# Attention on one Trainium2 core: a pair's eight sums over keys, in one group or in two

## What is computed

```python
sim = jnp.einsum('bhid,bhjd->bhij', qn, kn)            # 4 heads of 64, 1024 queries, 1101 keys
sim = jnp.where(full_mask[:, None, None, :], sim, neg)
attn = jax.nn.softmax(sim.astype(jnp.float32), axis=-1).astype(sim.dtype)
out = jnp.einsum('bhij,bhjd->bhid', attn, v)
out = out.transpose(0, 2, 1, 3).reshape(b, nl, INNER)
return out @ W_out + b_out
```

## Time and profile before

| | us |
|---|---|
| median of three runs | 876.07 |
| the three runs | 872.5, 883.99, 876.07 |
| profiled execution, first to last instruction | 875.4 |
| TensorE busy in it | 802.4 |
| VectorE busy | 546.3 |
| GpSimd busy | 373.1 |
| ScalarE busy | 366.9 |

### The profile page before, as it was taken

The page is one execution under the profiler, slowest core; times in us unless marked ns, Lnnn a source line. Parts: engine busy times, 40 slices in busy tenths (PEclk is TensorE's granted clock), DMA queues, the critical chain, the costliest instruction groups (busy, mean ns, idle before and its releaser), DMA issues.

```text
span 875.4 us, 13801 instructions
## 1 busy us (share of the span) xinstructions
PE 802.4 (92%) x4270; PEld 612.4 (70%) x4271; DVE 546.3 (62%) x1173; ACT 366.9 (42%) x1175; POOL 373.1 (43%) x396
## 2 busy tenths in 40 slices
PE   6888799999999899989999999999998799999995
PEld 4555445555555555548888878888886689999994
DVE  4958765777677756675998667777766433333331
ACT  4457133544354332344444366776660032222220
POOL 7256553344447364345475044444442312222221
PEclk9999599989899988999999999999998799999998
DMA  8580000000000000003600093000001364555520
GB/s 303 170 307 35 1 0 1 1 1 0 1 1 1 0 1 1 0 1 111 255 1 0 1 301 104 12 19 13 14 12 61 101 266 176 182 180 176 174 80 3
DMA packets 31887, 67.14 MB, mean 77 GB/s; under 512 B 3103, under 2 KB 22909, under 8 KB 30813
## 3 DMA queue, kind: packets, MB, share of 16 engines
q1 hardware_dynamic: 28699, 56.17, 18.3%
q0 software_dynamic: 2560, 10.17, 3.6%
q10 hardware_dynamic: 578, 0.19, 0.1%
HBM read 54.74 MB, written 12.68 MB: 77 GB/s over the span
## 4 chain that ended last, share of the span: by engine, by line
PE 67%; DVE 17%; issue 6%; ACT 3%; POOL 3%; DMA 2%; DVEq 0%; SPq 0%; ACTq 0%; POOLq 0%
PE PS L2105 9%; PE PS L2093 9%; PE PS L1488 7%; PE PS L734 6%; PE PS L1468 6%; PE PS L1296 5%; PE PS L1274 3%; PE PS L725 3%; PE PS L771 3%; PE PS L701 3%; PE PS L726 2%; DVE row_best L846 2%; PE PS L743 2%; POOL rrms L551 2%; ACT pc L1670 1%
## 5 line engine op out<-in xcount | busy, mean ns | idle before, releaser
L1055 ACT ACTIVATE EX<-PS 128x512 f32<-128x512 f32 x144 | 78.9, 594 | 133.4 <-PE PS L726 130.6
L846 DVE TENSOR_REDUCE row_best<-PS 128x1 f32<-128x1024 f32 x64 | 77.8, 1221 | 41.8 <-PE PS L701 41.5
L1015 POOL TENSOR_TENSOR sumP<-sumP,EX 128x1024 f32<-128x1024 f32 x32 | 75.7, 2364 | 43.1 <-ACT EX L1055 42.7
L1670 ACT ACTIVATE pc<-PS,mx 128x77 f32<-128x77 f32 x256 | 78.8, 359 | 26.8 <-DVE mx L1565 26.8
L2093 PEld LDWEIGHTS PS<-xeT,w 128*128 128x128 f32 x736 | 85.6, 192 | 3.6 <-DMA w<-in_L_ffn_W 1.3
L2093 PE MATMUL PS<-xeT,w 128*128 128x128 f32 x736 | 86.1, 275 | 2.0 <-DMA w<-in_L_ffn_W 1.1
L2105 PE MATMUL PS<-w,heT 128*128 x368 | 83.3, 379 | 1.3 <-DVE oe L2035 1.3
L2132 POOL DMA_INDIRECT out<-oe,target x23 | 23.2, 1011 | 126.1 <-DVE oe L2035 126.1
L734 PE MATMUL PS<-EX,V 128*64 128x512 f32 (+1 forms) x288 | 76.5, 640 | 0.0
L2105 PEld LDWEIGHTS PS<-w,heT 128*128 128x128 f32 x368 | 68.1, 190 | 10.0 <-issue 1.7
L1488 PE MATMUL PS<-vw,pcT 128*128 128x256 f32 (+1 forms) x320 | 73.0, 383 | 1.2 <-ACT pcT L1683 1.2
(11 more groups left out here) (283 smaller groups left out, 1716.1 us busy)
## 6 DMA issues: line engine op xcount, KB each, us to landing
w<-in_L_ffn_W SPq DMA_DIRECT2D x31, 1024.0 KB, 10.1
vw_rows<-vwn SPq DMA_DIRECT2D x2, 1232.0 KB
kwH_rows<-kwH SPq DMA_DIRECT2D x1, 2464.0 KB, 7.4
kwL_rows<-kwL SPq DMA_DIRECT2D x1, 2464.0 KB, 13.7
kwH<-kwH_rows POOLq DMA_DIRECT2D x1, 2464.0 KB, 12.3
kwL<-kwL_rows POOLq DMA_DIRECT2D x1, 2464.0 KB, 19.2
vw<-vw_rows SPq DMA_DIRECT2D x2, 1152.0 KB, 13.3
XR<-in_x SPq DMA_DIRECT2D x4, 512.0 KB, 13.4
```

The lines of the kernel that those rows point to most:

```text
L846: dve.tensor_reduce(row_best[:, n % 2, t // GT, t % GT:t % GT + 1], PSf[:, 512 * at:512 * at + S], AX.X, ALU.max, negate=True).then_inc(ma ...
L1015: pool.tensor_tensor(sumP[:], before, EX[:, (KT * n + c) % EB, :, :], ALU.add).then_inc(pool_summed, 1)
L1055: act.activation(EX[0:r, k % EB, i, :], PS[0:r, ST_AT + i, :], ACT.Exp).then_inc(exp_done, 1)
L1670: last = act.activation(pc[:, p, h * C:h * C + C], PS[:, 1 + part, (h - h0) * C:(h - h0) * C + C], ACT.Exp, bias=mx1[:, p, h:h + 1], accum ...
```

## The change

The eight sums of a pair are made in two groups of four products (eight instructions each): the query tiles 0 and 1 of both heads in step 1 of the next pair, tiles 2 and 3 in step 3, behind the context scores. The output products of tiles 0 and 1 lie between the groups, in step 2. Each group has a use of its own in the ring of spare banks and its own reciprocals on VectorE (in step 1, and in step 3 behind `both_max`). The tail's groups lie behind chunks 1 and 2. Waits on `sum_done` count two groups for a pair.

```diff
-    TAIL_SUM, TAIL_OUT = 1, (3, 5)
+    TAIL_SUM, TAIL_OUT = (1, 2), (3, 5)
...
-                if n > 0 and c == 1:
-                    yield "sum", n - 1, 0
+                if n > 0 and c in (1, 3):
+                    yield "sum", n - 1, c // 2
...
         yield "sum", PP - 1, 0
+        yield "sum", PP - 1, 1
...
-        def sums(n):
-            k0 = open_bank(pe, "sum", n, 0)
+        def sums(n, half):
+            k0 = open_bank(pe, "sum", n, half)
             pe.wait_ge(dve_summed, 3 * n + 3)
             for i in range(2):
-                for s in range(GT):
-                    last = pe.matmul(PS[:, k0, i * GT + s:i * GT + s + 1],
+                for s in (2 * half, 2 * half + 1):
+                    last = pe.matmul(PS[:, k0, i * 2 + s % 2:i * 2 + s % 2 + 1],
                                      sumD[:, i, s * P:s * P + P], onecol[:], start=True, stop=True)
             last.then_inc(sum_done, 1)
...
-                    if c == 1:
-                        sums(n - 1)
+                    if c in (1, 3):
+                        sums(n - 1, c // 2)
...
             if n > 0:
-                dve.wait_ge(sum_done, n)
+                dve.wait_ge(sum_done, 2 * n)
...
-        def reciprocals(n):
-            dve.wait_ge(sum_done, n + 1)
-            bank_read(dve.reciprocal(rl[:, n % 2].rearrange("p i s -> p (i s)"),
-                                     PS[:, bank_of("sum", n, 0), 0:2 * GT]), "sum", n, 0)
+        def reciprocals(n, half):
+            dve.wait_ge(sum_done, 2 * n + half + 1)
+            bank_read(dve.reciprocal(rl[:, n % 2, :, 2 * half:2 * half + 2],
+                                     PS[:, bank_of("sum", n, half), 0:4].rearrange("p (i s) -> p i s", i=2)), "sum", n, half)
...
             dve.wait_ge(proj_done, 2 * n + half + 1)
+            wait_read(dve, "sum", n, half)
             if half == 0:
-                wait_read(dve, "sum", n, 0)
                 dve.wait_ge(bias_added, BG * batch_of(n) + group_of(n) + 1)
...
-                if n > 0 and c == 1:
-                    reciprocals(n - 1)
+                if n > 0 and c in (1, 3):
+                    reciprocals(n - 1, c // 2)
```

More of the change, by code:

```diff
@@ L838, in pe_attend @@
                     values(n, done)
-        return {TAIL_SUM: lambda: sums(PP - 1), TAIL_OUT[0]: lambda: project_out(PP - 1, 0),
+        return {TAIL_SUM[0]: lambda: sums(PP - 1, 0), TAIL_SUM[1]: lambda: sums(PP - 1, 1), TAIL_OUT[0]: lambda: project_out(PP - 1, 0),
                 TAIL_OUT[1]: lambda: project_out(PP - 1, 1)}
@@ L1001, in dve_attend @@
         sum_both(PP - 1)
-        return {TAIL_SUM: lambda: reciprocals(PP - 1), TAIL_OUT[0]: lambda: add_out(PP - 1, 0),
+        return {TAIL_SUM[0]: lambda: reciprocals(PP - 1, 0), TAIL_SUM[1]: lambda: reciprocals(PP - 1, 1), TAIL_OUT[0]: lambda: add_out(PP - 1, 0),
                 TAIL_OUT[1]: lambda: add_out(PP - 1, 1)}
```

## The result

The changed kernel takes 872.75 us (median of 20 runs, 869.28 to 878.75); the kernel before, in the same rounds, 880.7 (872.5 to 884.56). The ratio is 0.9913, 95% interval [0.9891, 0.9935]: 0.9% faster, surely faster and well inside two per cent. The forecast was 865.2, in the range 859 to 877. The direction and the range held.

What follows compares the result with a forecast made beforehand. The prediction took TensorE, slowed by clock falls in attention, to bound the kernel. From 875.4 us, 11.0 us of clock time back and 0.8 us paid for group starts gave 865.2 us, range 859 to 877.

Steps and rivals of the forecast that it cites:

- What bounds the kernel: Whole kernel: TensorE, busy 92% of the span, sets the pace and loses part of it to clock dips in attention.
- What a fall costs: Attention boundaries: 0.455 us lost per us at half clock, 15.7 us for five falls holding 34.5 us at 1.2 GHz.
- the one on the clock: Boundaries between attention pairs: with halved groups only boundary 5 still falls, 15.7 - 4.7 = 11.0 us back.
- the 1.8 that held: Boundary 7: 1.8 us of one-column products without a wait kept full clock, taken as the yardstick for other boundaries.
- Nobody waits for VectorE there: VectorE, steps 1 and 3: one more reciprocal a pair, 0.207 us, and its earlier place in step 1 change nothing.
- Sums in two groups: Steps 1 and 3: same 64 products; step 1 loses 0.9 us and step 3 gains 0.9, net nothing.
- their start: Second group's start, new eight times: 8 x 0.1 = 0.8 us paid, bounds 0 and 4 us.
- the ring: Three spare banks, one more use in step 3: waits covered, 0 us; up to 2.8 us kept for the range.
- The rivals: Other outcomes for the clock: 860.5 us (chance 0.20), 876.2 us (0.20), about 887 us (0.08).
- The second thin place: Step 3: narrow context products plus new group, 1.4 us, make the clock fall; 22 us cost, about 887; chance 0.08.
- The indifferent clock: Attention boundaries: waits beside the sums decide, every fall stays, 876.2 us; chance 0.20.
- The base: Profiled span of 875.4 us that the terms were summed against; the three runs' median is 0.7 us above.

Runs made afterwards that it cites:

- maximum first: Groups in step 2 ahead of the row scores and in step 3, with VectorE's row maximum moved ahead of the last key tile's sum in step 0: 863.72 us, 0.9806.
- one group behind values: Kernel before, its unsplit group of sixteen instructions moved within step 1 from ahead of the values to behind them, reciprocals in step 2: 866.82 us, 0.9865.
- the addition held: Kernel before, with GpSimd's addition of the third key tile in pair 7 waiting for VectorE's four normalizations: 874.63 us, 0.9956.

## Why the prediction was right or wrong

**What bounds the kernel**, TensorE and its clock: right. Versions that do the same TensorE work with a third less time at 1.2 GHz are 16 to 20 us faster, and some two thirds of that go with the clock by the line (12.8 of 18.7 us in the run with groups in steps 2 and 3).

**What a fall costs**: 0.455 us per us at half clock came from two pairs of windows of one execution; over all runs it is 0.373. The five falls of the profiled execution were worth 12.9 us then, not 15.7.

**The step that failed** is the one on the clock: "Boundaries 1, 3 and 6 come under the 1.8 that held, and I count them as held." All three fell, and so did 4. The rule that I drew, that thin work of up to 1.8 us holds, rested on one boundary in one execution; 1.8 us of sums with no wait ahead fell in the run with one group in step 2, and waits without sums fell too. What the runs show in its place: halving a group that stays behind its two waits does little (five falls in the one profile before and in the one after, 34.5 and 37 us; 8.8 us less at 1.2 GHz over all runs); taking it away from behind them does much (29.8 us less). Of the 11.0 us on this term, the runs give 8.8 x 0.373 = 3.3 us at most, since a part of the 8.8 may belong to pair 7.

**A term that was missing**: 2.6 us in pair 7. "VectorE ... Nobody waits for VectorE there" looked at what is queued behind the new reciprocal. It didn't follow what the 0.8 us longer step 3 puts off: the next numerators, GpSimd's next addition, and through it VectorE's normalizations, for which TensorE had waited 2.43 us before. 3.3 and 2.6 make 5.9 of the 6.7 us between the means (879.5 over 50 runs, 872.8 over 20); 0.8 is not accounted for, or 1.6 against the mean of the 20 runs of before in the same rounds (880.3).

**Sums in two groups, their start, the ring**: right. Groups of eight take 0.9 to 1.0 us; the second one has no idle time ahead of it except 0.24 us in pairs 2 and 4, the wait that the item had; the item behind it waits no longer. In pair 2, though, where the clock held, TensorE came to step 2's item sooner and waited 1.35 us for VectorE's `add_out`, 0.60 at the same place of pair 4: part of what the clock gives back is lost there.

**The rivals**: in the profile of the change no fall began in step 3. The second thin place exists, but it is rare: among the 42 groups in step 3 of seven profiles the clock fell behind two (pair 2 of the run with groups in steps 2 and 3, pair 4 of "maximum first"). The Trainium skill's rule that was named beside it ("TensorE: Matmul & The Clock Gate", section "A second HAM failure mode: psum-queue depth-cycling") is not borne out here as what decides: the versions with groups in steps 2 and 3 use as many banks as the change and are the fastest that do all the work, 0.9784 and 0.9774. The indifferent clock was half right: at boundaries 2, 4 and 5 the waits alone were enough in one execution, and at boundary 5 the clock fell ahead of the sums, behind the 0.9 us wait, in three profiles (the change, one group behind values, maximum first). The Trainium skill's rule on idle gaps (same page, section "HAM oscillation — how this bites in real kernels") points the same way, though the waits of its example are longer than these. The other half it doesn't reach: moving one group from ahead of the values to behind them took 21 us of half clock away, while the idle time of TensorE in pairs 1 to 6 went only from 13.2 to 12.6 us.

**The base**: the three runs given had a median of 876.07; 50 runs have 878.9. That, and the 1.8 us around the span, make the forecast of 865.2 look further off than its terms were.

**Left open**: the runs with the split in pair 7 only and with the addition held have 5.6 us less at 1.2 GHz than before, though neither touches boundaries 1 to 6. A part can be the fall behind the 2.4 us wait of pair 7, which both remove (3.4 us in two of the four profiles that have the wait); a part can be scatter, which is about 4 us on this difference. So how much of the change's 3.3 us is due to boundaries 1 to 6 is not settled: about 1 us if all of the 5.6 belongs to pair 7, up to 3.3 if none does. And what in a stretch of waits and narrow products makes the clock fall is not shown: either can be enough, and the runs only show that keeping them apart helps.

## What to carry to other kernels

Where a clock falls at short, narrow products, look at what stands next to them: moving the narrow group behind wide work that is there anyway was worth 10 us here, with the wait ahead of it; halving it in its place was worth 3 at most. A clock that falls by luck has to be read from many runs' clocks, not from one trace's windows. And an edit that only delays one step by a microsecond can pay or cost elsewhere, where one engine stands still for another, as VectorE's normalizations did here beside GpSimd's additions.

## What the runs showed of the hardware

A VectorE normalization of 128x256 takes 0.40 us alone and up to 2.60 beside a GpSimd addition of 2.4 us; the instructions of this line over the whole kernel before, ns min/median/max:

```profile
L1371 DVE TENSOR_SCALAR Z<-XR,mvg,rsg x16: 402/409/2603, 374.3 to 444.5; 128x256 f32<-128x256 f32 x16
```

The Trainium skill, "SBUF — State Buffer", section "Who interferes with whom", says that VectorE in a mode with two ports and GpSimd take a shared pair of ports in turn, and that whichever issues later is blocked for the whole of the other's instruction; it counts `tensor_scalar`, which the normalization is, among those that can enter such a mode. The trace doesn't show the mode, but it agrees with the blocking: in the kernel before, the two long normalizations (2.60 and 2.43 us) each end some 0.15 us after the addition beside them, and with the addition held the four take 1.62 us.

And in the changed kernel TensorE's clock fell from 2.4 to 1.2 GHz at boundaries where no idle piece ahead of the fall was longer than 0.91 us. TensorE was busy for 218.67 of 231.89 us in pairs 1 to 6.
